# Another layout of the q and k scratch in DRAM, between two transfers of a decoder block

## The reference

```
q = (query @ Wq.T + bq).reshape(B, T, H, D).transpose(0, 2, 1, 3)
k = (key @ Wk.T + bk).reshape(B, S, H, D).transpose(0, 2, 1, 3)
v = (value @ Wv.T + bv).reshape(B, S, H, D).transpose(0, 2, 1, 3)
scores = jnp.einsum('bhtd,bhsd->bhts', q, k) * scale
scores = scores + attn_mask[None, None, :, :]
...
scores = scores + spatial_bias + directional_bias
probs = jax.nn.softmax(scores, axis=-1)
out = jnp.einsum('bhts,bhsd->bhtd', probs, v)
return out.transpose(0, 2, 1, 3).reshape(B, T, E) @ Wo.T + bo
```

## Time and profile before

| | us |
|---|---|
| median of 3 timed runs | 2268.11 |
| lowest and highest | 2265.85, 2270.70 |
| span of the profiled execution, first to last instruction | 2269.1 |
| PE busy in it | 2080.3 (92%) |
| ACT, DVE, POOL busy | 2024.8, 1862.2, 1781.9 |
| mean share of the 16 DMA engines, q1 | 72.8% |

### The profile page before, as it was taken

One profiled execution on the slowest core, in us unless ns is written; L12 is line 12 of the kernel. 1 busy time (PEld: TensorE's weight loads), 2 busy tenths in 40 slices (PEclk: granted clock), 3 DMA queues, 4 the chain that ended last, 5 costly groups with the idle time before them and its releaser, 6 DMA issues.

```text
span 2269.1 us, 73067 instructions
## 1 busy us (share of the span) xinstructions
PE 2080.3 (92%) x24128; PEld 1807.7 (80%) x24128; DVE 1862.2 (82%) x6768; ACT 2024.8 (89%) x5937; POOL 1781.9 (79%) x1899
## 2 busy tenths in 40 slices
PE   4679999999999999999999999999999999999876
PEld 3458888888888888888888888888888888788755
DVE  4578888888888888888888888888888888888863
ACT  5589999999999998999999999999999999899862
POOL 2358888788888877888888888888888888788773
PEclk9789999999999999999999999999999999999998
DMA  4387778688777779776766887777788688788760
GB/s 144 109 182 162 164 164 174 158 170 190 169 158 164 168 155 180 175 160 160 174 167 160 188 180 161 169 164 172 155 183 182 161 160 169 150 164 186 167 135 19
DMA packets 711784, 367.16 MB, mean 162 GB/s; under 512 B 561392, under 2 KB 659952, under 8 KB 711408
## 3 DMA queue, kind: packets, MB, share of 16 engines
q1 hardware_dynamic: 711408, 362.50, 72.8%
HBM read 202.98 MB, written 25.17 MB: 101 GB/s over the span
## 4 chain that ended last, share of the span: by engine, by line
PE 57%; issue 13%; POOL 11%; ACT 8%; DMA 6%; DVE 4%; SPq 1%; ACTq 0%; POOLq 0%; DVEq 0%
PE ps_c_hidden L972 14%; PE ps_c_out L972 13%; PE ps_a_misc L972 13%; DMA b_probsT_hi_lo<-b_probs_hi_lo 5%; PE ps_b_misc L1109 5%; POOL bias L516 3%; PE ps_b_scores L1095 3%; PE ps_a_misc L1051 2%; POOL ctxT_hi L482 2%; ACT c_relu L678 2%; POOL a_qT_lo L474 2%; ACT ps_b_probs L652 2%; POOL ctxT_lo L485 2%; ACT a_qT_hi L597 2%; PE ps_a_scores L1032 1%
## 5 line engine op out<-in xcount | busy, mean ns | idle before, releaser
L516 POOL TENSOR_TENSOR bias<-bias,b_mask 128x512 f32<-128x512 f32 x512 | 644.8, 1274 | 6.2 <-DMA bias<-in_bias 5.8
L832 DVE CUSTOM_DVE_ANT_0 b_neg_scores<-ps_b_scores,bias 128x256 f32<-128x256 f32 x1024 | 391.6, 420 | 70.3 <-POOL bias L516 34.9
L839 DVE TENSOR_TENSOR b_probs_hi_lo<-ps_b_probs,b_probs_hi_lo 128x512 f16<-128x512 f32 x512 | 352.3, 688 | 106.0 <-ACT b_probs_hi_lo L660 103.6
L537 POOL TENSOR_TENSOR c_hidden_lo<-c_hidden,c_hidden_hi 128x512 f16<-128x512 f32 x288 | 335.1, 1164 | 48.4 <-issue 32.7
L972 PE MATMUL ps_c_hidden<-c_xT_hi,w_hi 128*128 128x256 f16 x1152 | 316.8, 275 | 20.2 <-ACT c_relu L678 20.2
L530 POOL TENSOR_TENSOR c_hidden<-c_relu 128x512 f32<-128x512 f32 x288 | 300.2, 1042 | 32.1 <-ACT c_relu L678 12.7
L972 PE MATMUL ps_c_out<-w_hi,c_hidden_hi 128*128 128x256 f16 x1152 | 315.3, 274 | 9.9 <-DVE acc L943 9.9
L972 PE MATMUL ps_c_hidden<-c_xT_lo,w_hi 128*128 128x256 f16 x1152 | 316.3, 275 | 0.0
L972 PE MATMUL ps_c_hidden<-c_xT_hi,w_lo 128*128 128x256 f16 x1152 | 316.3, 275 | 0.0
L972 PE MATMUL ps_c_out<-w_lo,c_hidden_hi 128*128 128x256 f16 x1152 | 315.5, 274 | 0.0
L972 PE MATMUL ps_c_out<-w_hi,c_hidden_lo 128*128 128x256 f16 x1152 | 315.4, 274 | 0.0
(11 more groups left out here) (194 smaller groups left out, 7498.1 us busy)
## 6 DMA issues: line engine op xcount, KB each, us to landing
bias<-in_bias SPq DMA_DIRECT2D x256, 512.0 KB, 4.4
q_stack<-qk_scratch SPq DMA_DIRECT2D x256, 64.0 KB, 2.6
x_ln<-in_x SPq DMA_DIRECT2D x32, 256.0 KB, 4.5
ctxT<-in_ctx SPq DMA_DIRECT2D x32, 256.0 KB, 4.5
x<-in_x SPq DMA_DIRECT2D x32, 256.0 KB, 5.3
qk_scratch<-b_qT_hi_lo SPq DMA_DIRECT2D x32, 256.0 KB, 4.6
qk_scratch<-b_kT_hi_lo SPq DMA_DIRECT2D x32, 256.0 KB, 3.8
k_stack_even<-qk_scratch SPq DMA_DIRECT2D x128, 64.0 KB, 2.5
```

The costliest lines, as they stand in the source:

```text
L516: gp.tensor_tensor(part, part, b_mask[:, :], ALU.add).then_inc(b_c_ok, 1)
L537: gp.tensor_tensor(c_hl[:, u, :], c_h[:, :], c_hh[:, u, :], ALU.subtract).then_inc(c_h_ok, 1)
L832: last = dve.tensor_tensor_reduce(out=b_t[:, u, c, :], in0=ps_bs[:, c * T:(c + 1) * T], in1=bias[:, slot, at:at + T], scale=-2.0, scalar=3 ...
L839: dve.tensor_tensor(b_p2[:, j % DEPTH, :, 1, :], ps_bp[:, :].rearrange("p (c t) -> p c t", c=CT), b_p2[:, j % DEPTH, :, 0, :], ALU.subtrac ...
```

## The change

The scratch gets another order of its dimensions: the row of a head (0 to 31, for two heads of 16) comes first, then the chunk `m`, then the pair of heads inside the chunk. The 8 pieces of 512 B that one row of a stack is made of lie next to each other, as 4 KB. On the side of the store, partition `p * 32 + hd` of the tile now goes to place `[hd, m, p]`. That pattern has one dimension more, and the store is made in two DMAs, one for hi and one for lo, of 128 KB each. The counts that wait for a store go from 16 to 32 a batch. Bytes, values, order of the steps and the engines' other instructions are the same.

```diff
             def b_store_k(b, _):
...
-                sp.dma_start(stk_d[1].rearrange("r m p t -> p r m t"), b_k2[:, :, :, :]).then_inc(b_k_dram, 16)
+                for r in range(2):
+                    sp.dma_start(stk_d[1, r].rearrange("hd m p t -> p hd m t"), b_k2[:, r, :, :]).then_inc(b_k_dram, 16)
             def b_store_q(b, _):
...
-                sp.dma_start(stk_d[0].rearrange("r m p t -> p r m t"), b_q2[:, :, :, :]).then_inc(b_q_dram, 16)
+                for r in range(2):
+                    sp.dma_start(stk_d[0, r].rearrange("hd m p t -> p hd m t"), b_q2[:, r, :, :]).then_inc(b_q_dram, 16)
             def stacked(kind, part, head):
-                return stk_d[kind, part].rearrange("m (p h d) t -> h d (m p) t", h=2, d=BD)[head]
+                return stk_d[kind, part, head * BD:(head + 1) * BD].rearrange("d m p t -> d (m p) t")
             def b_stack_k(b, _):
-                sp.wait_ge(b_k_dram, after(b, 16, 16))
+                sp.wait_ge(b_k_dram, after(b, 32, 32))
...
-    args.append(nc.dram_tensor("qk_scratch", (2, 2, CD, P, T), F16, kind="Internal").ap())
+    args.append(nc.dram_tensor("qk_scratch", (2, 2, 2 * BD, CD, P // (2 * BD), T), F16, kind="Internal").ap())
```

More of the change, by code:

```diff
@@ L401, in b_stack_q @@
             def b_stack_q(b, _):
-                sp.wait_ge(b_q_dram, after(b, 16, 16))
+                sp.wait_ge(b_q_dram, after(b, 32, 32))
                 carry_waits(sp)
@@ L490, in b_split_k @@
                 gp.wait_ge(b_kf_ok, after(b, 2, 2))
-                gp.wait_ge(b_k_dram, after(b, 16, 0))
+                gp.wait_ge(b_k_dram, after(b, 32, 0))
                 gp.tensor_tensor(b_k2[:, 1, :, :], b_kf[:, :, :], b_k2[:, 0, :, :], ALU.subtract).then_inc(b_kl_ok, 1)
@@ L497, in b_split_q @@
                 gp.wait_ge(b_qf_ok, after(b, 2, 2))
-                gp.wait_ge(b_q_dram, after(b, 16, 0))
+                gp.wait_ge(b_q_dram, after(b, 32, 0))
                 gp.tensor_tensor(b_q2[:, 1, :, :], b_qf[:, :, :], b_q2[:, 0, :, :], ALU.subtract).then_inc(b_ql_ok, 1)
@@ L626, in b_kv @@
                 act.wait_ge(b_k_ps, after(b, 1, 1))
-                act.wait_ge(b_k_dram, after(b, 16, 0))
+                act.wait_ge(b_k_dram, after(b, 32, 0))
                 for m in range(CD):
@@ L633, in b_q @@
                 act.wait_ge(b_q_ps, after(b, 1, 1))
-                act.wait_ge(b_q_dram, after(b, 16, 0))
+                act.wait_ge(b_q_dram, after(b, 32, 0))
                 for m in range(CD):
```

## The result

The changed kernel takes 2325.59 us (median of 4 runs, 2317.68 to 2333.21), the kernel before 2266.98 beside it (4 runs, 2264.64 to 2270.70). The ratio is 1.0266 with an interval of 1.0233 to 1.0298: slower by 58.6 us. The forecast was slower, by 109 us. The time lies in the range and in the likeliest case's own one. In the profiled executions the span goes from 2269.1 to 2315.9, +46.8. That is less than 58.6 because the two profiled executions lie at opposite ends of the scatter. The changed kernel's is its fastest of four (2317.68 us, a time 1.8 us over its span). With the same 1.8 the one of before stands at about 2270.9, 3.9 above its median and at the upper end of its runs.

A forecast was written before the change was run, and what follows sets the result against it. PE was taken to bound the kernel, idling for transpose 15 queued behind the q store. 31 rounds x 2.73 x 1.25 = 106 us plus 3 for the first batch gave +109, 2377 us, range 2300 to 2466.

The forecast's parts named there:

- the likeliest case: Whole kernel: store on four engines and transpose 15 on the path, 2377 us, own range 2300 to 2450, chance 0.76.
- A: The forecast's mechanism: q store on four engines, transpose 15 behind it late by 2.73 us, PE idle at it.
- The reads: Stack reads with one 4-KB packet for eight of 512 B: nobody waits for them, gain on the path 0.
- The second issue: Two store issues for one on SP, +0.48 us each for q and k, covered by existing waits: taken as 0.
- C: The theory that the second issue on SP, putting transpose 15 later, makes most of the 59 us: 2300 to 2325.
- The write pattern: New store's DRAM side: 128 packets on each of four engines, 3.64 us in place of 0.91, +2.73 us.
- the forecast's lower bound: Transpose 15's queue takes up all but 1 us of the delay: 31 x 1.05 = 33, 2301 us.
- The factor of 1.25: Round time lost per transpose delay, chosen between 1.05 and 1.67: 31 rounds x 2.73 x 1.25 = 106 us.
- The first batch: First batch, nothing running beside it: PE waits for the stacks themselves, +3 us.
- The stacks come level: Path from q store through stack reads to PE's next first scores: comes level, adds 0, up to 2 us a batch.
- The signs named: Changed profile: 57,344 fewer packets, 4 small per store, transpose 15 at 8 us, its wait 108 us, round 69.7 us.
- a possibility for the stacks: SP's issues held up until the k store has drained, delaying the stack reads: up to 2 us a batch.

The follow-up runs named there:

- Two issues: Kernel before, old store pattern, but each q and k store cut into two DMAs, hi and lo: 2261.66 us against 2262.66, ratio 0.9994.
- The reads alone: Kernel before with its old stores, stacks read as 4-KB rows (wrong values): 2261.06 us against 2263.39, ratio 0.9988.
- transpose first: Changed kernel with transpose 15 issued ahead of the q store on SP: 2328.63 us against 2262.66 for the kernel before, ratio 1.0289.
- four writes: New layout with hi and lo inside a head's row, each tensor written by four DMAs of 32 partitions: 2300.25 us against 2262.66 for the kernel before.
- eight blocks: Changed kernel with blocks of 16 rows, store's outermost count 8, reads in 512-B pieces: 2342.07 us against 2262.66 for the kernel before, ratio 1.0357.
- The old layout with an empty front: Kernel before with the context load moved ahead of transpose 12 and the last bias load behind the stack reads: 2245.37 us against 2263.11, ratio 0.9919.

## Why the prediction was right, and where its size was not

**The place.** A is shown. Most of the loss is PE's wait on L1109, now L1111; it appears with the q store alone, goes when the packets on the four engines are halved, and goes from that wait when the transpose is put ahead of the store.

**The reads: 0.** Right: alone they change nothing (0.9988, interval around 1), and their issue on SP stays at 0.42 us.

**The second issue: 0.** Right, and C is refuted (0.9994). With the new pattern an issue costs 0.58 us instead of 0.38, though, so that two take 1.2; the q_stack's reads come 1.9 us later, forecast were 3.

**The write pattern: four engines, 128 packets, 3.64 us.** Right on the engines, and on the time to 0.3 us or so.

**The step that failed is the size of this term.** "128 x 28 ns = 3.64 us in place of 32 x 28 = 0.91, that is +2.73 us" was mis-sized on the side of the old store. The 0.91 was read from a store alone; in a round its packets start over 1.87 us, and over 1.12 when the two loads in front of it are moved away. That the loads keep the engines at work unevenly, so that not all 16 get free at once, fits this, but no view tells the engines apart. The end of the store moved by 5.86 - 4.20 = 1.66 us in place of 2.73. Behind it the transpose's last packet follows after 0.96 us and not 1.27, and the semaphore after 0.76 and not 0.93. So 1.66 - 0.31 - 0.17 = 1.18 in this pair. The 0.31 and 0.17 are in part the long execution of before: against the two other runs with the old store the sum is 1.50 and 1.57. All of these lie nearer to the 1 us that the forecast's lower bound leaves of the delay than to 2.73.

**The factor of 1.25.** It came out near: 46.8 / (31 x 1.18) = 1.28 in the spans, and 58.6 / (31 x 1.5) = 1.26 for the medians with the lateness against "Two issues" (1.20 with the 1.57 against "The reads alone"). There was luck in it, since it was a choice between 1.05 and 1.67, the second from two single rounds. In the spans PE's idle alone makes 34.8 / 36.6 = 0.95 of it; the rest is PE busy longer with the same work, at a lower granted clock. Of the changed kernel's four runs the longest has the lowest clock: 0.971 in the shortest, 0.963 in the longest.

With 1.18 in the sum, 31 x 1.18 x 1.25 + 3 gives 48.7 us, 2317 in place of 2377; with 1.5 it gives 61, 2329. The measured 2325.59 lies between.

**The first batch: +3.** The first round is 65.1 us after and 62.2 before, so 2.9 longer. The reason given, the stacks, is only a part of it: PE reaches that batch's first scores 0.75 us later. The number came true, its mechanism for the most part was not shown.

**The stacks come level: 0.** Right: 2.1 us of wait at the first scores, 0.6 before. It was near, though. Every variant that took the transpose off the four engines' tail but left the store late (transpose first, four writes, eight blocks) lost at just this place.

**The signs named.** Packets less 57,344: seen. Small packets 4 per store: seen. Transpose 15 at 8 us from its own issue: it was 6.7 in the batch shown and 6.3 on the mean. The wait of 108 us: 59.7. The round of 69.7: 67.8. All of these misses go back to the one size.

**The better order.** The old layout with an empty front beats both kernels, 0.8% below the kernel before. The profile before had shown 24.9 us that it could win, the two other runs with the old store about 18; 17.7 came.

## What to carry to other kernels

Look at the outermost count of both sides of a DMA before changing a layout: here it set how many of the 16 engines share the packets, and four engines with 128 packets each cost more than 57,344 packets saved. Price a transfer by its time in the flow in front of the waiter, not by its time alone; what it replaces can be slower there than on an idle queue. Before a difference of a few microseconds is split into terms, see where in the scatter of its kernel each profiled execution lies. And where a wait stands behind a transfer queue, see first what is issued just in front: moving two loads gained 17.7 us here, while no layout tried gained anything.

## What the runs showed of the hardware that wasn't expected

**SP's next issue takes longer behind 128 packets on each of four engines.** The issue of transpose 15 takes SP 1.76 us on the mean behind the old store and 3.86 behind the new, with the same instruction; with 64 packets on each of the four or eight engines it is 1.84 and 1.79. It starts 0.83 us later and ends 2.93 later, and everything behind it in SP's list waits. The forecast had seen this only as a possibility for the stacks. How much of the transpose's lateness is its own longer issue, and how much its packets' wait on the four engines, these runs don't separate.

**The time of an issue goes by its pattern.** On SP the store of 128 x 4 pieces takes 0.38 us, the stores with outermost counts of 4, 8 and 32 take 0.58, 0.63 and 0.60, though they have half of the pieces or fewer; the reads take 0.43, 0.42 and, in the layout of eight blocks, 0.60.

**The granted clock can fall behind an idle of about 2 us.** In the kernel before, the round with the late transpose, view of windows (PE, PEld, DVE, ACT, POOL, then the granted clock, DMA's share, GB/s):

```profile
889.40:897.90 8.50, 5.94 (x86) 5.45 (x84) 6.14 (x26) 6.03 (x20) 6.67 (x6) 1.00 1.01 198
897.90:906.00 8.10, 8.07 (x77) 7.22 (x78) 5.99 (x20) 5.66 (x19) 2.38 (x2) 0.79 0.90 115
897.80:901.20 3.40, 3.27 (x29) 2.85 (x30) 2.27 (x8) 0.90 (x2) 0.79 (x1) 0.51 0.85 137
```

Right behind the 2.68 us of idle the clock was at the lower of its two levels, 1.2 GHz, for 3.4 us, and PE was busy in nearly all of them. As an estimate, half of the 3.4 is lost, and 2.68 + 1.7 = 4.4 us is what this round lost, 4.48. Two such stretches of the kernel after, each behind a wait for transpose 15 of 2.0 and 1.8 us:

```profile
371.00:374.40 3.40, 3.40 (x30) 2.90 (x27) 2.29 (x8) 1.20 (x3) 1.14 (x2) 0.50 0.63 186
575.80:579.20 3.40, 3.40 (x21) 2.79 (x19) 2.50 (x9) 2.04 (x6) 1.98 (x2) 0.50 0.63 183
```

The idles of the changed kernel are 1.9 us long on the mean and come in every batch, but the clock doesn't fall behind each of them. Between 160 and 2160 us, the part where all stages run, it falls in 7 rounds after and in 2 before, each time within some 1.2 us of the end of such an idle of 1.7 to 2.7 us; behind the other idles of the same length it stays up. Five stretches more of 3.4 us make 17 us at the lower level, so an estimated 8.5 us lost. The rest of the 12.6 us of busy time lies at the start and the end of the kernel, where the clock is low for longer in the profile after as well. That an idle causes a fall was read in such rounds, not tested by an experiment, and what decides which idle does stays open.
